# Spreading the attention denominators of two transformer stacks: a selector matmul on TensorE replaced by a lane shuffle on VectorE

## What is computed

```python
H, HD = 16, 8                       # heads, width of a head
def _attn(q, k, v, mask):
    scores = jnp.einsum('bqhd,bkhd->bhqk', q, k) / np.float32(np.sqrt(HD))
    scores = jnp.where(mask[:, None, None, :], -jnp.inf, scores)
    w = jax.nn.softmax(scores, axis=-1)
    return jnp.einsum('bhqk,bkhd->bqhd', w, v)
...
a = _attn(q, k, v, src_mask).reshape(B, L, D) @ so_w[i].T    # self, 512 keys
x = x + a
...
a = _attn(q, k, v, ctx_mask).reshape(B, L, D) @ co_w[i].T    # cross, 154 keys
x = x + a
xn = _adaln(x, noise_emb, n3_w[i], n3_b[i])
h = jax.nn.gelu(xn @ f1_w[i].T + f1_b[i], approximate=False)
x = x + (h @ f2_w[i].T + f2_b[i])
```

## Time and profile before

| | |
|---|---|
| median of 3 runs | 3533.99 us (3525.29 to 3542.89) |
| profiled execution, its own time | 3528.05 us |
| its span, first to last instruction | 3526.2 us |
| busy share of the span: PE, DVE, ACT, POOL | 85%, 59%, 54%, 23% |
| mean granted PE clock | 0.947 of full |

### The profile page before, as it was taken

The page is one execution under the profiler, slowest core; times in us unless marked ns, Lnnn a source line. Parts: engine busy times, 40 slices in busy tenths (PEclk is TensorE's granted clock), DMA queues, the critical chain, the costliest instruction groups (busy, mean ns, idle before and its releaser), DMA issues.

```text
span 3526.2 us, 44923 instructions
## 1 busy us (share of the span) xinstructions
PE 2989.9 (85%) x15735; PEld 1049.5 (30%) x15735; DVE 2086.3 (59%) x3631; ACT 1909.0 (54%) x2693; POOL 805.7 (23%) x1327
## 2 busy tenths in 40 slices
PE   7998999868888788888888856888888888888878
PEld 3463333222222222222222222222222222222226
DVE  4326777448375664846658266658375674746634
ACT  5433333337566574665647534647566575665642
POOL 0003454502212222222212102212212122212211
PEclk9999999879999999999989977989999999999999
DMA  1100000001110111101011001011110111101020
GB/s 42 55 14 11 1 1 1 11 20 42 33 37 27 42 28 32 45 20 51 23 33 41 22 9 45 21 35 41 35 37 27 36 34 32 43 22 51 19 94 38
DMA packets 125514, 110.11 MB, mean 31 GB/s; under 512 B 49982, under 2 KB 116076, under 8 KB 125292
## 3 DMA queue, kind: packets, MB, share of 16 engines
q1 hardware_dynamic: 114924, 97.80, 9.4%
q10 hardware_dynamic: 10368, 9.44, 0.9%
HBM read 41.96 MB, written 0.52 MB: 12 GB/s over the span
## 4 chain that ended last, share of the span: by engine, by line
PE 62%; DVE 19%; ACT 7%; POOL 5%; issue 4%; ACTq 1%; SPq 1%; DMA 0%; DVEq 0%; POOLq 0%
PE ps L514 11%; DVE arena L797 9%; PE ps L459 6%; PE ps L488 4%; PE ps L645 4%; ACT arena L670 3%; PE ps L587 3%; PE ps L630 3%; PE ps L543 2%; PE ps L531 2%; PE ps L573 2%; DVE arena L799 2%; PE ps L1491 2%; PE ps L522 2%; PE ps L1479 2%
## 5 line engine op out<-in xcount | busy, mean ns | idle before, releaser
L670 ACT ACTIVATE arena<-ps 128x1024 f32<-128x1024 f32 x960 | 936.4, 1024 | 352.5 <-PE ps L488 349.5
L797 DVE TENSOR_REDUCE arena<-ps 128x1 f32<-128x512 f32 x1536 | 965.4, 684 | 173.2 <-PE ps L459 160.7
L514 PE MATMUL ps<-arena 128*32 128x512 f32 x3840 | 512.5, 608 | 21.2 <-ACT arena L670 18.0
L459 PE MATMUL ps<-arena 49*128 49x512 bf16 x1536 | 312.0, 403 | 226.4 <-DVE arena L797 198.6
L488 PE MATMUL ps<-arena 52*128 52x512 bf16 x1920 | 346.1, 387 | 31.8 <-ACT arena L670 27.1
L799 DVE TENSOR_REDUCE arena<-ps 128x3 f32<-128x462 f32 (+1 forms) x576 | 303.4, 580 | 86.8 <-PE ps L466 81.2
L879 POOL TENSOR_TENSOR arena<-arena,zeros 128x16 bf16<-128x16 f32 x192 | 42.3, 220 | 1011.1 <-DVE arena L797 582.5
L459 PEld LDWEIGHTS ps<-arena 49*128 49x128 bf16 x1536 | 75.1, 94 | 557.8 <-DVE arena L797 479.2
L889 POOL TENSOR_TENSOR arena<-arena 128x512 f32<-128x512 f32 x96 | 121.9, 1270 | 450.7 <-ACT arena L702 450.7
L895 POOL TENSOR_TENSOR arena<-arena 128x512 bf16<-128x512 f32 (+1 forms) x84 | 92.4, 1100 | 549.9 <-ACT arena L729 549.9
L808 DVE TENSOR_TENSOR h<-ps,h 128x512 f32<-128x512 f32 x48 | 33.2, 692 | 291.8 <-PE ps L543 291.8
(11 more groups left out here) (383 smaller groups left out, 4280.3 us busy)
## 6 DMA issues: line engine op xcount, KB each, us to landing
arena<-arena SPq DMA_DIRECT2D x720, 64.0 KB
arena<-we_dram SPq DMA_DIRECT2D x24, 578.5 KB, 7.5
arena<-arena ACTq DMA_DIRECT2D x144, 64.0 KB
w<-weights_dram SPq DMA_DIRECT2D x26, 320.0 KB, 3.1
w<-weights_dram SPq DMA_DIRECT2D x13, 512.0 KB, 4.0
arena<-arena SPq DMA_DIRECT2D x384, 6.0 KB
arena<-arena SPq DMA_DIRECT2D x288, 19.2 KB
w<-weights_dram SPq DMA_DIRECT2D x39, 128.0 KB, 2.2
```

What stands on the lines that cost most here:

```text
L459: pe.matmul(s_bank(slot + r), qst[b][rows, idx, P * qt:P * (qt + 1)], kst[b][rows, idx, :], start=True, stop=True).then_inc(s_full, 1)
L514: mm = pe.matmul(bank(7)[32 * j:32 * j + 32, :], v, prob[:, slot, j, :], start=(g % 2 == 0 and kt == 0), stop=(a == 0 and g % 2 == 1 and k ...
L670: act.activation(prob[:, chunk_no(b, a, g, kt) % NPROB, 2 * p:2 * p + 2, :], e_bank(slot).rearrange("p (j n) -> p j n", j=2), ACT.Exp, sca ...
L797: op = ve.tensor_reduce(nmax[:, g % 2, r, n:n + 1], s_bank(slot + r), AX.X, ALU.max, negate=True)
```

## The change

The item `sel` keeps its number in the table, and moves from PE to DVE. In place of the matmul, DVE shuffles lanes within each block of 32 partitions: rows 0 to 15 all take row 8, rows 16 to 31 all take row 24, from `osb` straight into `rlog` in SBUF. ACT takes the logarithm in place there. The item no longer uses a slot of the "e" ring. The two selector matrices and their making (two memsets, two copies and a DMA, once) are gone. The hunks below are, in this order, the item's count, PE's part (removed), ACT's two parts, DVE's part (new) and SP's DMA at the start.

```diff
-            "evac": {"evac": 1}, "sel": {"e": 1}, "inv": {"inv": 1},
+            "evac": {"evac": 1}, "sel": {"sel": 1}, "inv": {"inv": 1},
...
-            def sel(it):
-                _, b, a, e = it
-                slot, at = z.use("e", it)
-                pe.wait_ge(v_free, z.after("evac", ("evac", b, a, e), it))
-                pe.wait_ge(e_free, z.room("e", it, 1))
-                pe.matmul(e_bank(slot)[:, 0:S], selector2[:, :], osb[:, e, :], start=True, stop=True)\
-                  .then_inc(e_full, 1)
...
             def sel(it):
                 _, b, a, e = it
-                slot, at = z.use("e", it)
-                act.wait_ge(e_full, at + 1)
-                act.wait_ge(den_inv, z.ahead("inv", it))
-                act.activation(rlog, e_bank(slot)[:, 0:S], ACT.Ln).then_inc(e_free, 1)
+                act.wait_ge(den_spread, z.after("sel", it))
+                act.activation(rlog, rlog, ACT.Ln).then_inc(den_log, 1)
...
             def inv(it):
-                act.wait_ge(e_free, z.after("e", ("sel", b, a, e), it))
+                act.wait_ge(den_log, z.after("sel", ("sel", b, a, e), it))
...
+            def sel(it):
+                _, b, a, e = it
+                ve.wait_ge(v_free, z.after("evac", ("evac", b, a, e), it))
+                ve.wait_ge(den_inv, z.ahead("inv", it))
+                ve.stream_shuffle(rlog, osb[:, e, :], [HD] * 16 + [16 + HD] * 16).then_inc(den_spread, 1)
...
-            sp.wait_ge(selectors_made, 4)
-            sp.dma_start(selector2[24:P:32, :], selector_right[8:P:32, :]).then_inc(selector_moved, 16)
```

More of the change, by code:

```diff
@@ L183, in steps @@
     return {"msplit": {"split": 4}, "turn": {"e": 1}, "tail": {"e": 1, "tail": 1}, "pv": {"pv": 1}, "pvt": {"pvt": 1},
-            "evac": {"evac": 1}, "sel": {"e": 1}, "inv": {"inv": 1}, "hi": {"hi": 1}, "out": {"s": 1}, "center": {"e": 1, "sq": 1},
+            "evac": {"evac": 1}, "sel": {"sel": 1}, "inv": {"inv": 1}, "hi": {"hi": 1}, "out": {"s": 1}, "center": {"e": 1, "sq": 1},
             "var": {"e": 1, "rstd": 1}, "apply": {"ln": 1, "scaled": 0 if item[-1] == 3 else 1}, "proj": {"s": 2, "rope": 1}, "vals": {"e": 1},
@@ L189 @@
 COUNTED = ["s", "e", "group", "hi", "c", "q0", "k0", "q1", "k1", "row0", "row1", "chunk", "tail", "ktail", "split", "pv", "pvt",
-           "evac", "inv", "sq", "rstd", "ln", "scaled", "rope", "first", "bias", "n0", "n1", "n2", "self", "cross", "sout", "cout", "ffn"]
+           "evac", "sel", "inv", "sq", "rstd", "ln", "scaled", "rope", "first", "bias", "n0", "n1", "n2", "self", "cross", "sout", "cout", "ffn"]
 class Stretch:
@@ L269, in build @@
         identb = sb("identb", [P, P], BF16)
-        selector2 = sb("selector2", [P, P])
-        selector_right = sb("selector_right", [P, P])
         rope = sb("rope", [P, 2, S])
@@ L333, in build @@
         w_loaded = {s: sem("w_loaded_" + s) for s in SECTIONS}
-        wout_zeroed, bias_ready, selectors_made, selector_moved = (sem(n) for n in (
-            "wout_zeroed", "bias_ready", "selectors_made", "selector_moved"))
+        wout_zeroed, bias_ready = sem("wout_zeroed"), sem("bias_ready")
         ktail_made = sem("ktail_made")
+        den_spread, den_log = sem("den_spread"), sem("den_log")
         s_full, s_free, e_full, e_free, v_free = (sem(n) for n in ("s_full", "s_free", "e_full", "e_free", "v_free"))
@@ L647, in f2 @@
                 mm.then_inc(s_full, 1)
-            does = {"score": score, "turn": turn, "exp": exp, "tail": tail, "pv": pv, "pvt": pvt, "sel": sel, "out": out,
+            does = {"score": score, "turn": turn, "exp": exp, "tail": tail, "pv": pv, "pvt": pvt, "out": out,
                     "center": center_h, "var": var, "proj": proj, "vals": vals, "gain": gain, "f1": f1, "f2": f2}
@@ L864, in f2 @@
                   .then_inc(s_free, 1)
-            does = {"score": score, "out": out, "apply": apply, "proj": proj, "gain": gain, "biasf": biasf, "f2": f2}
+            does = {"score": score, "out": out, "sel": sel, "apply": apply, "proj": proj, "gain": gain, "biasf": biasf, "f2": f2}
             for it, _ in z.order:
@@ L2464, in stack_pe @@
             pe.wait_ge(rows_made, 8)
-            pe.wait_ge(selector_moved, 16)
             pe.wait_ge(const_rows, 16 * 4 * B)
@@ L2539, in _ @@
             ve.memset(w[:, W_COUT:W_COUT + 2 * P], 0.0).then_inc(wout_zeroed, 1)
-            ve.memset(selector2[:, :], 0.0).then_inc(selectors_made, 1)
-            ve.memset(selector_right[:, :], 0.0).then_inc(selectors_made, 1)
             ve.wait_ge(consts_loaded, 16)
@@ L2544, in _ @@
             ve.tensor_copy(identb[:, :], ident).then_inc(ident_ready, 1)
[L2545 to L2548, removed]
             ve.wait_ge(bias_loaded, 16)
```

## The result

The kernel with the shuffle takes 3591.62 us (median of four runs, 3582.25 to 3597.22) against 3538.44 (3525.29 to 3544.48) for the kernel before, run beside it: a ratio of 1.0153, 95% interval [1.0113, 1.0192]. It is slower by about 53 us, where 29 were forecast. The profiled execution has a span of 3595.4 us (before 3526.2) and a mean granted clock of 0.921 (before 0.947).

A forecast was written before the change was run, and what follows sets the result against it. No engine alone bounds the kernel: PE has most of the chain, DVE's reductions 9%, the selector matmul 2%. Latency +3 and PE's clock +26 on the profiled 3528.05 gave 3557, or 3563 us against the median; range 3520 to 3600.

The forecast's parts named there:

- The price of a shuffle: On DVE, 128x512 f32 in SBUF: 0.69 us alone; queued 0.40 to 0.66 us, likeliest 0.60.
- Places 1 and 3, zero: Self-attention: PE is freed but then waits for DVE, whose shuffle stands ahead of the next reduction; no gain.
- Place 2, +0.2: Self-attention: the logarithm waits for the shuffle, so `att` and the `out` matmul come about 0.2 us later per layer.
- Places 4 and 5, -0.3 and -1.0: Per layer: `exp` gets its slot 0.3 us earlier at 4; PE saves 1.0 us at 5, shuffle hidden.
- Place 6, +1.0: Shuffle stands ahead of `apply` on DVE, so the projection starts near 2.0 us behind `evac`: 1.0 us lost per layer.
- Places 7 and 8, +0.6: Late logarithm and DMAs at 7, earlier logarithm at 8: together 0.6 us lost per layer, bounds +0.2 and +1.2.
- The latency sum, +3: Whole run, all places' latency terms together: +3 us; about -10 with a cheap shuffle, about +12 with a dear one.
- The clock, +26: PE's clock falls in two further low spells a layer at 1.1 us: +26 us, bounds 0 to 77 us.
- 1 (clock holds, 3537): Whole kernel: steps cancel, no further low-clock spells, 3537 us; chance 0.25.
- 2 (PE's time is kept): Short shuffle fits DVE's idle time, places 1 to 3 win 0.56 us each; -41 us, 3493 us; chance 0.12.
- 3: Clock drops everywhere: four further spells a layer and a dear shuffle, 3623 us; chance 0.13.
- 4: Small gain: a cheap shuffle and no further spells, -10 us, 3524 us; chance 0.05.

The follow-up runs named there:

- ghost_all: Changed kernel plus an unread filler matmul on PE at all 96 places: 3538.95 us, ratio to before 1.0020; second set 3543.66 us, 1.0027.
- double: Changed kernel with each shuffle done twice, the first into a scratch buffer: 3669.06 us, ratio to before 1.0379.
- order67_ghost5: Changed kernel, place 6's shuffle moved behind apply, place 7's ahead of the projection, fillers at places 1, 2, 3, 4, 8: 3490.71 us, ratio to before 0.9887.
- order6_ghost4: Changed kernel with place 6's shuffle moved behind apply and filler matmuls at places 1, 2, 3 and 8: 3524.42 us, ratio to before 0.9984.
- order7: Changed kernel with place 7's shuffle on DVE ahead of the next layer's first projection: 3580.21 us, ratio to before 1.0118.
- order67: Changed kernel with place 6's shuffle behind apply and place 7's ahead of the projection, no filler: 3570.36 us, ratio to before 1.0090.
- order6: Changed kernel with place 6's shuffle, logarithm and inverse moved behind apply: 3557.20 us, ratio to before 1.0074.

## Why the prediction held, step by step

**Direction and cause.** Right: slower, by the clock and not by the latency of the shuffle, and inside the range, 8 us from its upper end. The size was 53 us where 29 were forecast, and that is the clock term below.

**The price of a shuffle.** Taken as 0.69 us, measured 0.72 (717 to 754 ns); queued 0.60 taken, 0.62 measured. The Trainium skill ("VectorE: DVE Perf Modes", the perf-mode tier table) led to an estimate of 800 ns, and the row is 721.

**Places 1 and 3, zero.** Right in latency: -0.15 to +0.06 where the clock holds, -0.03 and +0.09 in ghost_all. `double` confirms the mechanism, that the shuffle fills the gap that the selector matmul had left.

**Place 2, +0.2.** Too small. After has +0.60, and the two traces of ghost_all still +0.52 and +1.10, with low clock behind place 2 for 48 and 72 us where before had 41 us. How much of that is `out` and how much clock was not separated.

**Places 4 and 5, -0.3 and -1.0.** Measured -0.24 and -0.97, the same in nearly every layer.

**Place 6, +1.0.** The wait is as worked out: projection at 1.97 us behind `evac`, 2.0 forecast, logarithm at 0.79, 0.78 forecast, in all layers. How much of it reaches place 7 was not separated: 6 to 7 changes by -0.87 to +2.69 us from layer to layer in after.

**Places 7 and 8, +0.6.** This sum was put together wrongly, though its parts were right. The logarithm of place 7 is 1.24 us late (1.2 forecast). That of place 8 stands at 0.80 and `out` 0.38 earlier (0.44 forecast). But the transfers, for which I kept a slack of 0.4 to 0.7 us, do not end last: the scores follow `out` directly. And of place 7's lateness only 0.5 us reach place 8 where the clock holds (ghost_all, +0.47 to +0.51 in most layers), not 0.8. So the latency of both is about +0.1 a layer, and not +0.6. What after shows there, +1.2 to +1.6 from 7 to 8, is that 0.5 and about 1.0 of low clock: its window from place 7 to place 8 has a granted clock of 0.88,

```profile
1611.92:1625.93 14.01, 11.18 (x54) 0.88 0.25 73
```

that of before 1.00:

```profile
1581.29:1593.80 12.51, 9.64 (x54) 1.00 0.26 78
```

In the last layers of the stacks, 7 to 8 is -0.72 in both, and with 0.38 at place 8 that makes -1.1 (-0.9 forecast).

**The latency sum, +3.** About right. ghost_all is +7 us, but its clock (0.954) is above that of before (0.947); its second set has the clock of before and is +10 us, and from place 5 to 6 alone the fillers cost 10. So little is left for latency; that it is just 3 isn't shown, and it comes out so although the terms of places 2, 7 and 8 were off.

**The clock, +26.** This is the term that was mis-sized: the fillers take 45 to 47 us away. I had two further spells a layer at 1.1 us, 24 in all. Counting unbroken stretches at the low level within the stacks by the last place before them, before has 12 behind place 2, 13 behind 6 and 15 behind 8, 40 in all and 191 us long together. After has 9, 12 and 10 behind places 1, 2 and 3, 13 and 10 behind 6 and 7, and 22 behind 8: 76, and 375 us. That is 36 more, three a layer, at 47 / 36 = 1.3 us. Places 1 and 3 came as said, 19 stretches, and by the table they cost 12 x (0.98 + 1.24) = 27 us, the whole of the forecast. Behind 4 there was none, and behind 6 as many as before. What the term left out is place 7 (ten stretches, about 1.0 us each) and the long stretch from 8 to the next layer's place 1: seven more, and longer, 167 us at the low level for 89, which the table has at 23 us. (The profiled execution is longer than the median, so these pieces add up to more than 47.) The step that was too small is "two a layer", read off places 1, 3, 4 and 6 without the waits behind 7 and 8. That places 1 and 3 alone come to the forecast's 26 is in part luck, since 4 and 6, which were named too, added nothing. The bounds of the term (0 to 77 us) held it, and the upper end of the range was drawn at three spells a layer, which is what came.

The Trainium skill ("TensorE: Matmul & The Clock Gate", a second HAM failure mode) says that micro-idles between groups of matmuls make the clock swing. The windows of place 1 and ghost_all agree, with 1.94 us against 1.07 for the same eight matmuls.

**PE's busy time.** "PE's busy time falls by about 107 us and the span does not" was wrong in its first half, and contradicts the prediction's own clock term: matmuls at half the clock are busy for longer. It fell by 14.7.

**Rivals.** 1 (clock holds, 3537) is what ghost_all is, 3539 and 3544: it needed the filler. 2 (PE's time is kept) did not come by itself, but order67_ghost5, at 0.9887 of before, takes as long (3493 was worked out for it, 3491 measured). That is a coincidence of sums: the gain there is of moved items at 6 and 7 and of fillers, and places 1 to 3, for which the rival had 0.56 us each, give none. 3 had four spells a layer and a dear shuffle: there were three, at 1.3 us and not 1.6, and the shuffle was not dear (0.72 us). 4 asked for a cheap shuffle and a clock that holds, and had neither.

**Open.** The stretch from 8 to 1 changes by -0.4 to +6.4 us from layer to layer within the stacks; its mean follows the clock, but which wait in it starts each spell was not isolated. Nor were the 6.5 us in front of the first place, in blocks that the change does not touch; ghost_all has 4.6 and 3.2 there in its two traces, and order6_ghost4, with the same blocks in front, -1.6, so it may be scatter of single executions.

## What to carry to other kernels

When work is taken off PE in a stretch where PE already waits for another engine, it may buy nothing and cost the clock of the next stretch; try the change with an unread filler matmul in the old one's place before judging it. And when an operation moves to another engine, its number in the order must be chosen anew: where it stood well for PE, it stood ahead of `apply` on DVE, and moving that one item gave back half of the loss, most of it through the clock.

## What was not expected of the hardware

- Low clock can move on. With places 1 and 3 filled, it came behind place 4 in eight of twelve layers (+1.38 us each), with the same instructions around place 4 and the same wait of 1.80 us as in a kernel where it never came (-0.24). In all there were 76 low stretches within the stacks in both, 334 us long for 375. Filling one wait can't be judged by that wait alone.
- A gain of latency can be returned by the clock further on, in part or in full: order7 took 1.76 us from 7 to 8 and lost 1.17 from 8 to 1; order67 against order6 took 1.74 and lost 2.50.
- Every shuffle is preceded by its own LOAD_MASK_SELECT of 11 to 15 ns, although the pattern is always the same. It has no cost that shows: two shuffles in a row still start 0.62 us apart.
- ACT's logarithm in place from SBUF takes 0.63 us, and took 0.60 from PSUM.
